# One-layer language model on one core: attention contexts stored without their zero quarters, and their product with the output weights run on quarter tiles of TensorE's array

## The reference

```python
qkv = x @ w_qkv
q, k, v = split into heads
q = softmax(q * SCALE, axis=-1)
k = softmax(k, axis=-2)
context = einsum('bnd,bne->bde', q, k)
out = einsum('bde,bnd->bne', context, v)
out = out.reshape(...) @ w_out + b_out
```

## Time and profile before

| | us |
|---|---|
| median of 3 runs | 840.93 |
| the three runs | 841.3, 838.04, 840.93 |
| span of the profiled execution | 833.9 |
| TensorE busy (matmuls) in it | 651.0 (78%) |
| VectorE busy | 478.1 (57%) |
| GpSimd busy | 341.2 (41%) |
| ScalarE busy | 322.7 (39%) |

### The profile page before, as it was taken

One profiled execution on the slowest core, in us unless ns is written; L12 is line 12 of the kernel. 1 busy time (PEld: TensorE's weight loads), 2 busy tenths in 40 slices (PEclk: granted clock), 3 DMA queues, 4 the chain that ended last, 5 costly groups with the idle time before them and its releaser, 6 DMA issues. The chain is left out here.

```text
span 833.9 us, 16489 instructions
## 1 busy us (share of the span) xinstructions
PE 651.0 (78%) x4836; PEld 561.4 (67%) x4837; DVE 478.1 (57%) x1161; ACT 322.7 (39%) x663; POOL 341.2 (41%) x307
## 2 busy tenths in 40 slices
PE   0029827999999999999999997117756789999991
PEld 0029825888887878888788876116646778898891
DVE  0026638577977778797777874724323444444440
ACT  0049303535343353534344344034423444444450
POOL 6704024141361717245171726333344545444442
PEclk9999958999999999999999999559879999999996
DMA  4570186001110201111020101432445444444442
GB/s 115 159 249 1 26 227 252 2 1 51 46 58 14 76 15 51 50 47 55 15 83 6 51 26 63 155 91 46 76 71 78 80 79 75 76 72 69 74 69 25
DMA packets 50386, 59.91 MB, mean 72 GB/s; under 512 B 13208, under 2 KB 46368, under 8 KB 49696
## 3 DMA queue, kind: packets, MB, share of 16 engines
q1 hardware_dynamic: 31200, 36.16, 15.0%
q0 software_dynamic: 14976, 22.10, 14.2%
q10 hardware_dynamic: 4160, 1.05, 0.6%
HBM read 31.59 MB, written 27.70 MB: 71 GB/s over the span
## 5 line engine op out<-in xcount | busy, mean ns | idle before, releaser
L1382 POOL DMA_INDIRECT out<-y,queue_rows x72 | 116.8, 1623 | 151.8 <-DMA out<-y,queue_rows 74.1
L645 POOL DMA_INDIRECT queue_d<-row,slot x64 | 65.0, 1015 | 163.2 <-DVE slot L966 146.1
L1464 DVE SCALAR_TENSOR_TENSOR act_w<-relu,queue_rows 128x512 f32<-128x512 f32 (+1 forms) x72 | 45.9, 638 | 140.7 <-ACT relu L1413 136.0
L1127 PE MATMUL bank<-xt_hi,w_first 128*128 128x512 f32 x256 | 94.6, 415 | 0.9 <-DVE second_half L840 0.9
L1127 PE MATMUL bank<-w_first,xt_hi 128*128 128x512 f32 x256 | 84.9, 413 | 3.5 <-DVE second_half L840 1.8
L695 ACT ACTIVATE second_half<-second_half 128x512 f32<-128x512 f32 x64 | 40.4, 631 | 121.0 <-DVE second_half L840 121.0
L637 POOL TENSOR_TENSOR second_half<-second_half,q_inv 128x512 f32<-128x512 f32 x64 | 64.8, 1041 | 44.6 <-DVE q_inv L849 44.4
L703 ACT ACTIVATE k_exps<-bank,k_negmax 128x512 f32<-128x512 f32 x64 | 44.1, 690 | 77.5 <-DVE k_negmax L856 77.4
L1505 PE MATMUL bank<-w_hi,a_hi 128*128 x228 | 71.5, 313 | 2.2 <-issue 1.9
L1505 PE MATMUL bank<-w_lo,a_hi 128*128 x228 | 64.8, 284 | 0.0
L1505 PE MATMUL bank<-w_hi,a_lo 128*128 x228 | 64.7, 284 | 0.0
(11 more groups left out here) (173 smaller groups left out, 1663.6 us busy)
## 6 DMA issues: line engine op xcount, KB each, us to landing
queue_rows<-queue_d SPq DMA_DIRECT2D x74, 129.0 KB, 2.2
store<-in_L_ffn_w SPq DMA_DIRECT2D x4, 1536.0 KB, 9.3
h_in<-h_d SPq DMA_DIRECT2D x9, 512.0 KB, 4.5
h_d<-store SPq DMA_DIRECT2D x8, 512.0 KB, 7.4
out<-res SPq DMA_DIRECT2D x8, 512.0 KB, 3.2
wqk<-in_L_attn_w_qkv SPq DMA_DIRECT2D x1, 2048.0 KB, 12.2
queue_d<-filler SPq DMA_DIRECT2D x9, 129.0 KB, 2.5
out<-y,queue_rows POOLq DMA_INDIRECT x72, 3.9
```

The costliest lines, as they stand in the source:

```text
L645: pool.indirect_dma_start(out=queue_d, in_=row[:, t, c, :], in_offset=None, out_offset=bass.IndirectOffsetOnAxis(ap=slot[:, TT * c + t:TT ...
L1127: last = nc.tensor.matmul(o, a, c, start=(n == 1), stop=(n == 3 * len(pairs)))
L1382: pool.indirect_dma_start(out=out, in_=y[:, u % 2, :], in_offset=None, compute_op=ALU.add, out_offset=bass.IndirectOffsetOnAxis(ap=rows[:, ...
L1464: nc.vector.scalar_tensor_tensor(out=act_w[:, u % 2, 0:width], in0=relu[:, u % 2, 0:width], scalar=rows[:, u, DIM:DIM + 1], in1=relu[:, u ...
```

## The change

`context` has no zero quarters any more: it is 128 partitions x 8 x 64, with one head of a pair in the lower and one in the upper 64 partitions, and its memset is gone. `context_take` is one instruction on 128 partitions. `g_of` is called twice, not four times, and each call takes 4 pairs: 16 matmuls of 64 rows and 64 columns, on the four quarters of the array (`tile_position=(DH * r, DH * x)`). Row half r reads partitions 64r to 64r + 63 and writes bank 2 + 2n + r; column half x writes partitions 64x to 64x + 63 of it. The four matmuls of an `i` differ in x and r.

So that the two heads of one 128-row block of `g` come from the same r, the heads are regrouped: context slot (a, r) holds head `head_at(a, r)`. The columns of the k weights are permuted as they are split (`by_rows`: three instructions in place of one, for the high and the low part), the rows of `wo` by four transfers in place of one, and `context_of` reads q at the head's place. `g_take` writes every other pair. `m_of` and all behind it are as before.

The second `g_of` stands behind `q_unit(6)`; the first one, ahead of it, now fills two banks, and the second waits for the copy of the first bank.

```diff
+def head_at(a, r):
+    return 4 * (a // 2) + 2 * r + a % 2
...
+    def by_rows(src, dst):
+        parts = [(src[:, 0:INNER], dst[:, 0:INNER])]
+        for r in range(2):
+            parts.append((src[:, INNER:].rearrange("p (j r x d) -> p r j x d", r=2, x=2, d=DH)[:, r],
+                          dst[:, INNER:].rearrange("p (j x r d) -> p r j x d", r=2, x=2, d=DH)[:, r]))
+        return parts
...
-            sp.dma_start(wo[:], w_out.rearrange("(a p) n -> p a n", p=P)).then_inc(wo_in, 16)
+            for r in range(2):
+                for c in range(2):
+                    sp.dma_start(wo[DH * r:DH * r + DH, c::2],
+                                 w_out.rearrange("(j r c e) n -> r c e j n", r=2, c=2, e=DH)[r, c]
+                                 ).then_inc(wo_in, 16)
...
-                nc.gpsimd.tensor_tensor(wqk_lo[:, k], wqk[:, k], wqk_hi[:, k].bitcast(F32), ALU.subtract
-                                        ).then_inc(wqk_lo_ready, 1)
+                for (src, high), (_, low) in zip(by_rows(wqk[:, k], wqk_hi[:, k]), by_rows(wqk[:, k], wqk_lo[:, k])):
+                    last = nc.gpsimd.tensor_tensor(low, src, high.bitcast(F32), ALU.subtract)
+                last.then_inc(wqk_lo_ready, 1)
...
-                nc.scalar.activation(wqk_hi[:, k], wqk[:, k], ACT.Copy).then_inc(wqk_hi_ready, 1)
+                for src, high in by_rows(wqk[:, k], wqk_hi[:, k]):
+                    last = nc.scalar.activation(high, src, ACT.Copy)
+                last.then_inc(wqk_hi_ready, 1)
...
-    context = sbuf("context", [P, PAIRS, P])
+    context = sbuf("context", [P, PAIRS, DH])
...
-            nc.gpsimd.memset(context[:], 0.0).then_inc(consts_pool, 1)
...
-                copy(g[:, 2 * n:2 * n + 2], tail_bank(2 + n)[:].rearrange("p (a n) -> p a n", a=2),
+                copy(g[:, 4 * (n // 2) + n % 2:4 * (n // 2) + 4:2], tail_bank(2 + n)[:].rearrange("p (a n) -> p a n", a=2),
...
-                for half in range(2):
-                    r = slice(DH * half, DH * half + DH)
-                    src = tail_bank(n)[r, 0:4 * DH].rearrange("p (a d) -> p a d", a=4)
-                    last = nc.vector.tensor_tensor(context[r, 4 * n:4 * n + 4, r], src,
-                                                   k_inv[r, 4 * n:4 * n + 4].unsqueeze(2).to_broadcast([DH, 4, DH]),
-                                                   ALU.mult)
-                last.then_inc(ctx_ready, 1)
+                nc.vector.tensor_tensor(context[:, 4 * n:4 * n + 4],
+                                        tail_bank(n)[:, 0:4 * DH].rearrange("p (a d) -> p a d", a=4),
+                                        k_inv[:, 4 * n:4 * n + 4].unsqueeze(2).to_broadcast([P, 4, DH]), ALU.mult
+                                        ).then_inc(ctx_ready, 1)
...
             def g_of(b, n):
-                pe.wait_ge(ctx_ready, b.nth(2, n // 2 + 1))
-                tail_free(b, 2 + n)
-                for a in range(2):
-                    last = nc.tensor.matmul(tail_bank(2 + n)[:, DIM * a:DIM * a + DIM], context[:, 2 * n + a],
-                                            wo[:, 2 * n + a], start=True, stop=True)
-                last.then_inc(tail_psum, 1)
+                pe.wait_ge(ctx_ready, b.nth(2, n + 1))
+                tail_free(b, 2 + 2 * n)
+                tail_free(b, 3 + 2 * n)
+                pe.sem_inc(pe_passed, 1)
+                for i in range(2):
+                    for x in range(2):
+                        for r in range(2):
+                            a = 4 * n + 2 * i + x
+                            last = nc.tensor.matmul(
+                                tail_bank(2 + 2 * n + r)[DH * x:DH * x + DH, DIM * i:DIM * i + DIM],
+                                context[DH * r:DH * r + DH, a], wo[DH * r:DH * r + DH, a], start=True, stop=True,
+                                tile_position=(DH * r, DH * x))
+                last.then_inc(tail_psum, 2)
...
                 g_of(prev, 0)
+                q_unit(b, 6)
                 g_of(prev, 1)
-                q_unit(b, 6)
-                g_of(prev, 2)
-                g_of(prev, 3)
                 q_unit(b, 7)
```

More of the change, by code:

```diff
@@ L238, in _ @@
             sp.dma_start(wqk[:], w_qkv.rearrange("(k p) n -> p k n", p=P)[:, :, 0:2 * INNER]).then_inc(wqk_in, 16)
-            sp.dma_start(wo[:], w_out.rearrange("(a p) n -> p a n", p=P)).then_inc(wo_in, 16)
+            for r in range(2):
[3 more added lines that the diff above has]
+                                 ).then_inc(wo_in, 16)
             sp.dma_start(bo_all[:], on_all(b_out)).then_inc(wo_in, 16)
-            sp.wait_ge(wo_in, 32)
+            sp.wait_ge(wo_in, 80)
             sp.wait_ge(conv_added, SETS)
@@ L492, in attend @@
         sem(n) for n in ("prob_exp_ready", "counted_ready", "rank_psum", "slots_ready", "queued"))
-    route_chain, logits_psum, logits_ready, dve_passed, pool_passed = (
-        sem(n) for n in ("route_chain", "logits_psum", "logits_ready", "dve_passed", "pool_passed"))
+    route_chain, logits_psum, logits_ready, dve_passed, pool_passed, pe_passed = (
+        sem(n) for n in ("route_chain", "logits_psum", "logits_ready", "dve_passed", "pool_passed", "pe_passed"))
     QK_USES, Q_UNITS, TAIL_USES = 2 + 2 * TT + PAIRS, 2 * TT, 12
@@ L602, in _ @@
                            ).then_inc(table.filler_ready, 1)
-            pool.wait_ge(consts_pool, 8)
+            pool.wait_ge(consts_pool, 7)
             nc.gpsimd.affine_select(out=before[:], in_=before[:], compare_op=ALU.is_gt, fill=0.0, base=0,
@@ L794, in _ @@
                                   ).then_inc(rw_copied, 1)
-            dve.wait_ge(consts_pool, 9)
+            dve.wait_ge(consts_pool, 8)
             def link(ins, chain, b, per, n, apart=False):
@@ L1081, in _ @@
             pe.wait_ge(rw_copied, 2)
-            pe.wait_ge(consts_pool, 9)
+            pe.wait_ge(consts_pool, 8)
             def first(b):
@@ L1167, in context_of @@
                     for t in range(TT):
-                        for half in range(2):
-                            c = P * (4 * n + a) + DH * half
+                        for r in range(2):
+                            c, d = P * (4 * n + a) + DH * r, DH * head_at(4 * n + a, r)
                             last = nc.tensor.matmul(
-                                tail_bank(n)[DH * half:DH * half + DH, DH * a:DH * a + DH], k[:, t, c:c + DH],
-                                q[:, b.par, t, c:c + DH], start=(t == 0), stop=(t == TT - 1),
-                                tile_position=(0, DH * half))
+                                tail_bank(n)[DH * r:DH * r + DH, DH * a:DH * a + DH], k[:, t, c:c + DH],
+                                q[:, b.par, t, d:d + DH], start=(t == 0), stop=(t == TT - 1),
+                                tile_position=(0, DH * r))
                 last.then_inc(tail_psum, 1)
```

## The result

| | before | after |
|---|---|---|
| median of 4 runs, us | 841.12 | 870.68 |
| least and most | 838.04 to 841.32 | 869.39 to 872.48 |
| span of the profiled execution | 833.9 | 870.2 |

The ratio is 1.0369, with an interval of 1.0334 to 1.0404: the change makes the kernel 3.7% slower, where it was forecast to be 0.9% faster. The profiled execution of after took 871.85 us.

What follows compares the result with a forecast made beforehand. TensorE and the VectorE-then-ScalarE chain were taken to reach `m_of` together, both full. Loop 5.2, first round 1.4 and last batch 0.9 sum to 7.5 us saved, from 840.93 to 833.4 us; range 829.5 to 840.0.

Steps and rivals of the forecast that it cites:

- So no new wait in the loop: At both `g_of` calls in the loop: the banks they need are freed in time, so no wait is added.
- GpSimd starts its rows a mere 0.43 sooner: Behind `m_of` in a loop round: GpSimd gains only 0.43 us, covered by its 2.91 us wait later in the round.
- The slow rival: `g_of`'s four tiles do not overlap at all: 3.56 us a call, 26 us lost, 867 us; chance 0.04.
- the column tiles of one row group run in turn: In `g_of`, tiles run only two at a time: 1.85 us a call, 839.8 us in all; chance 0.13.
- `g_of`: Quarter tiles on TensorE run four at a time: 1.0 us a call, 2.0 a batch, 1.4 saved.
- `context_take`: On VectorE, one instruction replaces two: 0.43 us saved, twice a batch, so later pieces come 0.86 us sooner.
- The weight split: ScalarE's split of the q/k weights into more instructions: 0.4 us dearer, covered by 0.96 us before `conv(8)`, costed at nothing.
- The first round: First batch, without routing: TensorE alone binds up to `m_of`, so the whole 1.4 us is saved.
- The last step: Last batch, nothing beside it: `m_of` starts at 506.2 in place of 507.08, 0.9 us saved.
- A round of the loop: From `q_unit(5)` to `m_of`: 0.86 us saved, not 1.4, the rest ending in waits for VectorE; six rounds 5.2 us.
- Behind `m_of` all hang on each other: The part of a loop round after `m_of`: no further saving counted there beyond the 0.86 us.
- rival 3: In the loop VectorE does not bind, so every round gives TensorE's 1.4 us: 829.7 us; chance 0.08.

Runs made afterwards that it cites:

- the interleaved kernels: The changed kernel and the kernel before, each with GpSimd's eight indirect transfers alternating with its eight `q_norm`: 828.45 us (ratio 0.9868) and 840.11 us (0.9999).
- before's kernel interleaved: The kernel before, with only GpSimd's eight indirect transfers of a round alternating with its eight `q_norm`: 840.11 us, ratio 0.9999.

## Why the prediction was wrong

**The step that failed** is "So no new wait in the loop". It asked of each bank and buffer who frees it and when, and that list was right: no data came late. It took for granted that a matmul's report follows its last pass by the 0.39 us of the trace of before. In after the second `g_of` of every round of the loop, 16 passes in 1.0 us under GpSimd's indirect transfers, reports 6.9 to 7.6 us after its last pass, so that `m_of` waits 4.5 us for ScalarE's `g` and then runs 2.6 us longer at the half clock. The prediction looked at GpSimd for its own work only ("GpSimd starts its rows a mere 0.43 sooner") and never asked what TensorE does meanwhile. Nothing in before's trace shows such a lag, so its size could not be read there. What could be read was that `enqueue` and `g_of` coincide, and that the passes would on the mean be four times as close. No rival had it.

**The slow rival's 867 us** lies near the 870.68, and its mechanism did not occur: a call takes 1.0 to 1.2 us, not 3.56, so the nearness is luck. Nor did the column tiles of one row group run in turn, which would make 1.85 us a call. The prediction drew that from the Trainium skill ("TensorE: Matmul & The Clock Gate", section "Part 3: Packing small matmuls"), which says only that a weight load overlaps running matmuls when its row group differs and not otherwise. The trace of after disagrees with that sentence as well: four passes start within 0.02 us from 269.80 on and the next four 0.25 us later, which with two row groups takes two column tiles of one group side by side, and the weight loads of the next four start at 269.85, under the passes in flight.

**The terms, as far as they can be seen.** *`g_of`*: 1.0 forecast, 1.02 to 1.21 measured. *`context_take`*: 0.42 us forecast, and the rows of line 887 have it (ns, least/median/most), against 0.86 the pair in the earlier trace rows:

```profile
L887 DVE TENSOR_TENSOR context<-bank,k_inv x16: 417/425/426, 165.8 to 534.8; 128x256 f32<-128x256 f32 x16
```

*The weight split*: 0.4 us dearer forecast; ScalarE's six pieces take 4.18 us where two took 3.82:

```profile
68.95 4.18 ACT L307 ACTIVATE w_first<-wqk 128x1024 fp32r<-128x1024 f32 x6
```

*The first round*: 1.4 forecast. From `g_of`'s start to `m_of` it was 7.57 us before (171.7 in the earlier trace rows to 179.27 in the earlier trace rows) and is 6.49 after (170.80 to 177.29), 1.1 less. *The last step*: 0.9 forecast; in the interleaved kernels the last two `m_of` stand 37.55 us apart with the change and 38.20 without, 0.65 less.

*A round of the loop*: 0.86 forecast, since TensorE's gain beyond it would end in waits for VectorE. With the reports on time it is 48.35 - 46.99 = 1.36 us (means of five rounds: 226.70 to 468.44 in before's kernel interleaved, 222.82 to 457.75 in the changed one). In the round that ends at 410.94, the stretch from `g_of` to `q_unit(6)` is 0.86 us shorter (404.95 - 403.67 = 1.28, against 414.32 - 412.18 = 2.14), that from there to `m_of` is the same 5.99, and both are as forecast. A further 0.58 came from the part between `m_of` and `g_of`, costed at nothing with "Behind `m_of` all hang on each other". TensorE waits 0.26 us for ScalarE's `k_exps` there in the kernel without the change and not with it; for the rest I have no row. So six rounds give 8.2 in place of 5.2, and with the first round and the last step 9.9 rather than the forecast 7.5. The medians differ by 11.7, near rival 3's 11.2, but its reason did not hold: VectorE did bind at `q_unit(6)`. For the remaining 1.8 us I have no row; the two profiled executions also differ by 2.6 us before the first `m_of` (176.10 and 178.74) and by 4.0 behind the last, where the code is the same.

## What to carry to other kernels

A change that replaces few long matmuls by many short ones can make TensorE's reports late. Look up which engine issues transfers in that stretch, above all GpSimd's indirect ones, and treat the delay from the last pass to the first dependent instruction as a quantity to measure after the change, since it isn't a constant. Where it has grown, try breaking the transfers up among the engine's other work: here that turned 3.7% slower into 1.3% faster, while neither delaying the transfers nor reporting differently did.

## What was not expected of the hardware

- While GpSimd issues indirect transfers back to back (eight, 1.27 us apart), a report of TensorE can have a lag of up to 7.6 us. The report was out between the fifth transfer and 1.6 us behind the last. Passes 0.216 us apart in `g_of` had a lag of 0.39 us under them; calls with passes 0.11 us apart (tiled or not), 0.12 and, as four quarter tiles, 0.05 us apart on the mean had 1 to 7.6 in the loop, but 0.3 to 0.8 in the last step. Whether the number of passes or their spacing counts was not separated. One indirect transfer at a time, with a 1.06 us norm between, left up to 1.0 us at `g_of`. The same bytes sent by SyncE, and direct transfers of GpSimd over 4.8 us, held nothing there; indirect ones over 4.9 us gave 2.6 to 2.7.
- Raising by 2 after tiled matmuls is dearer than two raises when the reports are held: 870.68 and 859.88 us. With the reports of `g_of` on time the two are 848.27 and 846.47, which is within noise.
- What inside the chip holds them **stays open**. Whether they would be held in an execution that isn't recorded **stays open** too: every run here was recorded. Of TensorE's semaphore events the record of before misses none of 649, that of after 11 of 633; but they are also missing where nothing is held (8 in the run with full matmuls and a raise by 2, 20 in before's kernel interleaved).
- The Trainium skill ("NOTIFIC — the notification-queue block", section "7.1 Overflow: three behaviours, one of which stalls the engine") says that the block which writes such records holds back its producers when its own pipeline fills. No run here shows whether that is what happened.
- Four 64 x 64 tiles run at a time: 16 passes of 256 columns give way after 1.02 us, against 3.41 for 16 in sequence.
